# Transformer kernel on one core: first chunk of x loaded alone and norms ahead of splits, last feed-forward jobs moved forward, lengths of keys and values as two chains

## The reference

```python
x = x + attn_a(layernorm(x))   # softmax attention, causal, 16 heads of 16 channels
x = x + ffn(layernorm(x))      # r * (relu(k)^2 @ W_v): xr, xk mix each token with the one before
x = x + attn_b(layernorm(x))   # causal; keys and values are scaled to length 1
x = x + ffn(layernorm(x))
```

## Time and profile before

| | us |
|---|---|
| three runs | 3007.73, 3010.7, 3011.09; median 3010.7 |
| profiled execution, own time | 3010.78 |
| its span, first to last instruction | 3009.1 |
| busy: TensorE, ScalarE, VectorE, GpSimd | 2862.4, 2232.7, 1472.8, 817.1 |
| mean granted TensorE clock | 0.976 of full speed |

### The profile page before, as it was taken

One profiled execution on the slowest core, in us unless ns is written; L12 is line 12 of the kernel. 1 busy time (PEld: TensorE's weight loads), 2 busy tenths in 40 slices (PEclk: granted clock), 3 DMA queues, 4 the chain that ended last, 5 costly groups with the idle time before them and its releaser, 6 DMA issues.

```text
span 3009.1 us, 99722 instructions
## 1 busy us (share of the span) xinstructions
PE 2862.4 (95%) x42984; PEld 1302.0 (43%) x42984; DVE 1472.8 (49%) x3579; ACT 2232.7 (74%) x2487; POOL 817.1 (27%) x1246
## 2 busy tenths in 40 slices
PE   6999999999999899998999999999999989999897
PEld 3444444444444344444444444444444434444343
DVE  5322346565556654445344434555665656523544
ACT  2799978787787478784788878778787856788472
POOL 4222223332323222221222222232333322322111
PEclk9999999999999899998999999999999999999898
DMA  5322312222222123222322223222222221222111
GB/s 136 106 83 81 95 53 78 70 73 67 81 71 60 52 67 103 81 76 67 95 81 74 82 89 94 64 78 68 63 75 71 73 66 52 72 72 85 41 62 41
DMA packets 229828, 225.34 MB, mean 75 GB/s; under 512 B 33221, under 2 KB 212933, under 8 KB 229320
## 3 DMA queue, kind: packets, MB, share of 16 engines
q1 hardware_dynamic: 228504, 217.47, 25.3%
q10 hardware_dynamic: 816, 0.79, 0.1%
HBM read 146.80 MB, written 71.32 MB: 72 GB/s over the span
## 4 chain that ended last, share of the span: by engine, by line
PE 72%; DVE 16%; issue 6%; ACT 4%; POOL 1%; SPq 0%; DVEq 0%; DMA 0%; ACTq 0%
PE ps L872 46%; PE ps L1103 23%; ACT probs L828 4%; DVE pmax L1434 3%; PE ps L884 3%; DVE xn L1198 2%; DVE nw_y L1180 1%; DVE nw_u L1178 1%; DVE ln_st L1186 1%; DVE nw_u L1176 1%; DVE x_buf L1315 1%; DVE o_blk L1493 1%; DVE k_blk L1413 1%; DVE nw_v L1389 1%; POOL buf_k L703 0%
## 5 line engine op out<-in xcount | busy, mean ns | idle before, releaser
L828 ACT ACTIVATE probs<-ps 128x1024 f32<-128x1024 f32 x2176 | 2083.1, 1059 | 477.7 <-PE ps L872 474.5
L872 PE MATMUL ps<-q_st,k_st 99*32 99x512 bf16 (+3 forms) x20480 | 1237.4, 349 | 5.0 <-issue 2.4
L1103 PE MATMUL ps<-probs,v_st 128*17 128x512 f32 (+3 forms) x10240 | 1160.7, 532 | 22.4 <-POOL probs L731 13.1
L872 PEld LDWEIGHTS ps<-q_st,k_st 99*32 99x32 bf16 x20480 | 567.0, 96 | 775.7 <-issue 449.6
L731 POOL TENSOR_SCALAR_AFFINE_SELECT probs<-probs 128x256 f32<-128x256 f32 (+1 forms) x896 | 433.4, 501 | 1138.7 <-ACT probs L828 1120.1
L1103 PEld LDWEIGHTS ps<-probs,v_st 128*17 128x17 f32 x10240 | 291.9, 98 | 272.2 <-issue 59.1
L872 PE MATMUL ps<-xT,wT 128*32 128x512 f32 x2048 | 242.6, 594 | 0.0
L1493 DVE STREAM_TRANSPOSE o_blk<-ps 128x512 f32<-128x512 f32 x128 | 91.0, 711 | 269.2 <-PE ps L1103 268.9
L657 POOL TENSOR_TENSOR parts<-rest,parts 128x512 bf16<-128x512 f32 x96 | 120.9, 1260 | 316.7 <-DVE parts L1221 316.7
L1348 DVE SCALAR_TENSOR_TENSOR buf_v<-buf_v,ps 128x512 f32<-128x512 f32 x64 | 44.0, 687 | 272.9 <-PE ps L872 272.9
L1315 DVE TENSOR_TENSOR x_buf<-x_buf,ps 128x512 f32<-128x512 f32 x64 | 43.8, 684 | 217.6 <-PE ps L872 207.2
(11 more groups left out here) (140 smaller groups left out, 2148.9 us busy)
## 6 DMA issues: line engine op xcount, KB each, us to landing
part_a<-parts SPq DMA_DIRECT2D x192, 128.0 KB
x_buf<-in_L_attn_a_X SPq DMA_DIRECT2D x32, 512.0 KB, 4.6
q_st<-part_a SPq DMA_DIRECT2D x128, 128.0 KB
o_chan<-o_out SPq DMA_DIRECT2D x64, 256.0 KB, 2.4
o_in<-o_chan SPq DMA_DIRECT2D x64, 256.0 KB, 4.6
q_st<-part_b SPq DMA_DIRECT2D x128, 128.0 KB
k_st<-part_a SPq DMA_DIRECT2D x64, 192.0 KB, 2.9
part_b<-parts SPq DMA_DIRECT2D x96, 128.0 KB
```

Of the source, the lines that this page charges most:

```text
L828: nc.scalar.activation(probs[:, g % NP_BUF, :], ps[:, bk:bk + 2, :].rearrange("p a n -> p (a n)"), ACT.Exp, scale=SCALE[ATT[g // (NHG * NG ...
L872: last = pe.matmul(o[c:c + 32], kt[:, c:c + 32], q, **how)
L1103: last = pe.matmul(ps[32 * j:32 * j + VW, bank, q0:q0 + w], v_st[:, k % 2, kb, hg * HG + j, :], p, start=(kb == 0), stop=(kb >= TB * qc), ...
```

## The change

1. **Prologue.** SyncE waits for the first chunk of x to land before it issues the second load and all that follows. In `T_P0` the loads go from offset -10 to -16 and the norm from 0 to -5, so the norm of chunk c+1 stands ahead of the splits of chunk c on VectorE; it waits until TensorE has read `xn` (`t1`).
2. **Last FFN jobs.** Starts 16, 37, 58, 82 become 10, 24, 45, 69; `o_in` is loaded at offset -4. The last job's second half of `o_in` is no longer stored to DRAM and loaded: VectorE's last transposition writes it, and TensorE waits on that.
3. **Lengths.** The chain of 128 columns becomes two of 64: the keys' chain at offset 58 of an MA job, with the multiplication of `k_blk` at its end (before: offset 69), and the values' chain at 64. GpSimd's multiplication of the values goes from 70 to 75.

```diff
-T_P0 = {"load": -10, "ln": 0, "t0": 6, "t1": 8, ...
+T_P0 = {"load": -16, "ln": -5, "t0": 6, "t1": 8, ...
-       "len": 63, "keys": 69, "split": 91, "vb": 70, "low": 94, "store": 98}
+       "klen": 58, "vlen": 64, "split": 91, "vb": 75, "low": 94, "store": 98}
+T_LAST = {**T_END, "o_load": -4}
-    jobs += [Job("MB", 3, c, 7, start(7, 3) + (16, 37, 58, 82)[c], T_END) for c in range(NCH)]
+    jobs += [Job("MB", 3, c, 7, start(7, 3) + (10, 24, 45, 69)[c], {**T_LAST, "load": -4} if c == 2 else T_LAST) for c in range(NCH)]
...
-            for c in range(2):
-                load_x(JOB["P", 0, c])
+            load_x(JOB["P", 0, 0])
+            sp.wait_ge(s_x[0], 16)
+            load_x(JOB["P", 0, 1])
...
+                        if j is LAST_JOB:
+                            pe.wait_ge(s_o_in, 32 * f + 16)
+                            pe.wait_ge(s_ot, len(ATT) * KT * NCH)
...
-                yield j.t0
+                yield j.t0 + j.off["ln"]
+                if j.b == 0 and j.c:
+                    dve.wait_ge(s_part, JOB["P", 0, j.c - 1].at["t1"].n + 1)
...
-                yield j.t0 + j.off["len"]
+                yield j.t0 + j.off["klen"]
                 nh = TB * H
                 dve.wait_ge(s_ksq, 2 * (j.at["ma"] + 1))
...
+                inverse_lengths(buf_a, of_keys)
+                fac = nw_v[:, of_keys]
...
+                step(nc.vector.tensor_tensor(keys, keys, fac.unsqueeze(2).to_broadcast([P, nh, DK]), ALU.mult))
+                settle()
+                yield j.t0 + j.off["vlen"]
                 dve.wait_ge(s_vsq, 2 * (j.at["ma"] + 1))
...
+                inverse_lengths(buf_k, of_values)
...
+                    dst = o_out[:, i % 2, :]
+                    if sg == NI * NCH - 1:
+                        dve.wait_ge(s_part, JOBS[-2].at["o1"].n + 1)
+                        dst = o_in[:, KT - 1, :]
```

More of the change, by code:

```diff
@@ L119 @@
        "flag": 31, "store": 4}
-T_P0 = {"load": -10, "ln": 0, "t0": 6, "t1": 8, "u0": 14, "u1": 16, "u2": 18, "u3": 20, "v0": 22, "v1": 24, "n": 28,
+T_P0 = {"load": -16, "ln": -5, "t0": 6, "t1": 8, "u0": 14, "u1": 16, "u2": 18, "u3": 20, "v0": 22, "v1": 24, "n": 28,
         "flag": 31, "store": 4}
@@ L237 @@
 JOB = {(j.kind, j.b, j.c): j for j in JOBS}
+LAST_JOB = JOB["MB", B - 1, NCH - 1]
+assert LAST_JOB is JOBS[-1]
 def stored(u):
@@ L455, in m_job @@
                 load_x(j)
+                if "o_load" in j.off:
+                    yield j.t0 + j.off["o_load"]
                 load_o(j)
@@ L481, in load_o @@
                 for m in range(KT):
+                    if j is LAST_JOB and m == KT - 1:
+                        continue
                     sp.wait_ge(s_o_out[j.c % 2], 16 * ((k * KT + m) * (NCH // 2) + j.c // 2 + 1))
@@ L1181, in rsqrt, with inverse_lengths @@
                     settle()
+            def inverse_lengths(sq, at):
+                step(nc.vector.tensor_reduce(nw_v[:, at], sq[:, :, :].rearrange("p k (g e) -> p (k g) e", e=DK), AX_X, ALU.add))
+                settle()
+                step(nc.vector.tensor_scalar(nw_v[:, at], nw_v[:, at], 1.0e-30, None, ALU.max))
+                settle()
+                rsqrt(at)
+                step(nc.vector.tensor_tensor(nw_u[:, at], nw_v[:, at], nw_y[:, at], ALU.mult))
+                settle()
+                step(nc.vector.tensor_scalar(nw_u[:, at], nw_u[:, at], NORM_EPS, None, ALU.add))
+                settle()
+                step(nc.vector.reciprocal(nw_y[:, at], nw_u[:, at]))
+                settle()
             def statistics(j, first, end):
@@ L1382, in m_job @@
                     nc.vector.memset(vT[:, :, 0:1], 0.0).then_inc(s_vlast, 1)
[L1383 removed]
+                yield j.t0 + j.off["klen"]
                 nh = TB * H
                 dve.wait_ge(s_ksq, 2 * (j.at["ma"] + 1))
[L1386 to L1393, removed]
[L1394 to L1405 removed]
+                of_keys, of_values = slice(0, nh), slice(nh, 2 * nh)
+                inverse_lengths(buf_a, of_keys)
+                fac = nw_v[:, of_keys]
                 step(nc.vector.tensor_tensor(fac.rearrange("p (k b h) -> p k b h", k=KT, h=2),
[L1407 removed]
+                                             nw_y[:, of_keys].rearrange("p (k b h) -> p k b h", k=KT, h=2),
                                              k_scale[:, :].rearrange("p (k h) -> p k h", h=2).unsqueeze(2)
                                              .to_broadcast([P, KT, BL, 2]), ALU.mult))
[L1410 removed]
                 settle()
@@ L1414, in m_job @@
                 settle()
+                yield j.t0 + j.off["vlen"]
+                dve.wait_ge(s_vsq, 2 * (j.at["ma"] + 1))
+                inverse_lengths(buf_k, of_values)
+                nc.vector.tensor_tensor(v_fac[:, :].rearrange("p (t h) -> p t h", t=TB),
+                                        nw_y[:, of_values].rearrange("p (t h) -> p t h", t=TB),
+                                        v_scale[:, :].unsqueeze(1).to_broadcast([P, TB, H]),
+                                        ALU.mult).then_inc(s_vfac, 1)
                 yield j.t0 + j.off["split"]
```

29 lines of the change are left out of this document (8 added, 21 removed).

## The result

| | before | changed |
|---|---|---|
| median of 5 runs, us | 3010.7 (3007.73 to 3011.5) | 3023.88 (3020.66 to 3025.72) |
| span of the profiled execution | 3009.1 | 3023.7 |

What follows compares the result with a forecast made beforehand. TensorE, busy 2555.65 of 2640 us, was taken to bound the kernel, leaving only idle time or clock to gain. Prologue, boundary and tail summed as 3010.8 - 7.7 + 2.4 + 5.7 = 3011.2, forecast 3011, range 2997 to 3023.

Steps and rivals of the forecast that it cites:

- Boundary: Boundaries between instances, 16 times, 14 with waits: +2.4 us in all, range -13 to +14.
- the third: Boundary: GpSimd's moved multiplication of the values (1.94 us) lies over the norm's chain, +0.95 at 3, +0.42 at 4, +0.22 at 4.
- The first step of the boundary: Boundary: keys done at 466.8, values' chain at 472.6 against 472.5 before, so the wait of `o1` stays, +0.1.
- both collisions with the squares: Boundary, keys' chain: VectorE slows beside GpSimd's two squarings of the values, 0.8 us charged twice.
- The second step: Boundary: `k_blk` multiplication no longer between the additions of `o0` and `o1`; products' wait of 2.49 falls to about 1.1.
- the third rival: Boundary: the keys' chain makes values' sum, `o1`, addition and L884 1.0 later at 14 places: 3025, chance 0.25.
- Prologue: Start, up to the first scores: -7.7 us, range -9 to -4, first scores near 83.
- The three gaps: Prologue: TensorE's three waits of 2.60 for the norm are taken away, -7.8 us.
- The parameters: Prologue: they arrive later behind SyncE's wait, +1.0; `head_row` issued at 13.0, 2.2 to arrive.
- Tail: Last FFN jobs and end: 18.9 added ahead of the last products, 13.2 less behind them, +5.7, range -6 to +12.
- The stalls for `o_in`: Tail: TensorE waits 4.5 us for c = 0 and 2.9 for c = 1, clock charged separately at 2.0 and 1.0.

Runs made afterwards that it cites:

- vb75: Kernel before with one number changed, GpSimd's multiplication of the values at 75 in place of 70: 3027.98 us, ratio 1.0058.
- best_vb79: `best` with GpSimd's multiplication of the values at 79: 2991.96 us, ratio 0.995.
- chains_vb70: Kernel before with the two chains of 64 columns, keys first, and GpSimd's multiplication of the values left at 70: 3004.67 us, ratio 0.9979.
- chains: Kernel before with the change's third part alone (two chains of 64, GpSimd's multiplication of the values at 75): 3029.15 us, ratio 1.0068.
- after_vb70: Changed kernel with GpSimd's multiplication of the values back at 70 in place of 75: 3001.79 us, ratio 0.9973.
- pro_norm20: Kernel before with norms ahead of splits and x loads at -20, without SyncE's wait for the first chunk: 3004.48 us, ratio 0.9979.
- jobs: Kernel before with the change's second part alone (last FFN jobs forward, last outputs kept on chip): 3013.74 us, ratio 1.0012.
- keys_late: Kernel before with keys only summed in idle time, values' chain next, keys' chain and `k_blk` multiplication at 85, values' multiplication at 70: 2977.45 us, ratio 0.9891.
- best: Kernel before with `keys_late`, `pro_norm20` and the second part at starts 14, 28, 52, 69 together: 2969.84 us, ratio 0.9868.
- best_vb83: `best` with GpSimd's multiplication of the values at 83: 2989.54 us, ratio 0.9929.

## Why the prediction was wrong, point by point

**Boundary: wrong, and this decides.** Forecast +2.4, measured +16.5. The step that failed is the third, in which I charged GpSimd's multiplication "up to its length, less the single-operand instructions it covers". That subtraction is false for `tensor_scalar`: an instruction with one operand was stopped until the multiplication ended as well (1.87 at 475.78, 1.37 in `vb75`, 1.88 in `best_vb79`), at 14 of the 16 boundaries of the changed kernel. The place was right: the multiplication was to lie at about 479.4 to 481.3, and began at 475.69 + 4.26 = 479.95. I had seen that statistics (`bn_stats`) beside that work keep their time, and took this for all instructions with one operand. I charged 2.9 + 1.7 + 0.9 = 5.5 for it, at 11 places; VectorE's instructions beside it are 26.5 longer, at 16. The runs that differ in this number alone measure, in the long stretch, 26.7 (`chains_vb70` to `chains`), 20.1 (before to `vb75`) and 22.2 (`after_vb70` to the changed kernel), 1.3 to 1.7 at each of 16 boundaries.

The first step of the boundary was half right. The keys were to be done at 466.8 in the time of before, and were at 462.44 + 4.26 = 466.7, with both collisions with the squares as charged (0.77 and 0.75). The values' chain was to end at 472.6 and ended at 469.06 + 4.26 = 473.3: beside the masks its instructions, `tensor_scalar` ones among them, are longer too (0.29 to 0.54 in place of 0.20 to 0.23). So `o1` waits 1.94, not 1.27. I had counted 14 boundaries for it; the earlier trace rows gives 14 for `o_blk`, and the 1.17 of `o1` stood at 12. The second step was right in kind: the products' wait fell by 8.7, and with `vb` at 70 that is a net gain: `chains_vb70` is 5.8 faster than before, its long stretch 7.1 shorter.

**The rival.** The time that came, 3024, is that of the third rival (3025, chance 0.25), but that is luck. The rival wanted the values' sum at 467.8, and it began at 462.47 + 4.26 = 466.7, as I had worked out; of its mechanism, a keys' chain that makes everything later, only the 0.8 of `o1` at 12 boundaries is there. The larger part is the place of the multiplication, which the rival did not have. What the Trainium skill, "SBUF — State Buffer", section "Who interferes with whom", states was worth more than I made of it. Beside instructions with two SBUF inputs it names `tensor_scalar` among those that can enter a two-port mode, when their operands meet its conditions, and then contend, and says that the one that comes second fully blocks. The traces agree: the small instruction ends within 0.03 us of the multiplication at 14 of 16 places in the changed kernel and at all 16 in `vb75`. I had weighed the rule for two-input instructions only.

**Prologue: right in kind, too large.** Forecast -7.7, measured -4.3 at the first scores. The three gaps went as forecast. The parameters cost 0.92 (+1.0 forecast), by luck: `head_row` went out at 11.40, not 13.0, and took 3.7 to land, not the 2.2 that I had estimated. The missing term is SyncE's queue: the fourth chunk's load stood behind loads that wait for stores, 3.14. But `pro_norm20` shows that this was not the last bound either; by its trace the stores of the parts come next. The size, from one execution of each kernel, holds over all of them: first scores at 85.6 to 87.9 in the three with the changed prologue, at 88.7 to 92.4 in the eight with the old one.

**Tail: right within its range.** Forecast 18.9 - 13.2 = +5.7, measured 14.4 - 11.9 = +2.5 (alone, `jobs`: +15.3 - 12.6 = +2.7). The stalls for `o_in` were 3.4 and 2.0 (forecast 4.5 and 2.9); after the last products 37.6 passed to the end, counted from the transposition (forecast 36.2 from the products). The loss is only in the starts: 14, 28, 52, 69 turn it into a gain.

**The sum.** -4.4 + 16.5 + 2.5 = +14.6 between the spans. Two terms of three were good to 3.3 us, the third was off by 14.

## What to carry to other kernels

Where two engines can stop each other, as VectorE and GpSimd do here, a long instruction of the one has a price that depends on what the other does at that moment, and a number in an order table moved it from free (0.6 us in all) to 20 us. Look in the trace for small instructions that take several times their usual time and end together with the other engine's; and read in the order whether a changed number moves anything at all. Give first what the next wait hangs on: the values first and the keys into a later idle stretch was worth 32 us, where cutting the chain in two with the keys first, at its best, was worth 6.

## What I had not expected of the hardware

A `tensor_scalar` on 128x4 elements takes 1.87 us beside a GpSimd multiplication of 1.93, and 0.17 alone; `bn_stats` in the same place keeps its time, and so does the addition with one operand in PSUM when it begins inside the multiplication (0.69 at 473.77 in `keys_late`, where the multiplication lies from 472.11 to 474.05). The same prologue took from 85.2 to 89.1 us to the first scores in one execution each of `pro_norm20`, `best`, `best_vb79` and `best_vb83`, which have it alike; what moves it is open.
